# Linear recurrence of an adaLN network: one drive product per group, its halves exchanged through SBUF

## The reference, cut to what matters

```
h = layernorm(x) * (1 + ca) + sa
lam = exp(-exp(nu_log) + 1j*exp(theta_log))
Bu  = (h @ (B_re + 1j*B_im).T) * exp(gamma_log)      # 64 complex states per token
s_t = lam * s_(t-1) + Bu_t                            # along the 1024 tokens
y   = real(s @ (C_re + 1j*C_im).T) + h @ D.T
x   = x + ga * y
h   = layernorm(x) * (1 + cb) + sb
x   = x + gb * (shared_expert(h) + routed_experts(h)) # 8 experts, the best 2 of them
```

## Time and profile before

| what | value |
|---|---|
| median of 3 runs | 548.56 us (548.49 to 548.58) |
| the profiled execution | 549.87 us, its span 548.1 us |
| TensorE busy | 494.0 us (90%) |
| VectorE busy | 427.0 us (78%) |
| ScalarE busy | 349.6 us (64%) |
| GpSimd busy | 339.3 us (62%) |
| DMA | 20.98 MB moved, mean 38 GB/s |

### The profile page before, as it was taken

How to read it: one execution, slowest core, us unless ns; L and a number is a source line. 1 busy time by engine, 2 the same in 40 slices (tenths; PEclk the granted TensorE clock), 3 DMA queues, 4 the chain that set the end, 5 groups by cost and what they waited for, 6 DMA issues and landing times.

```text
span 548.1 us, 11812 instructions
## 1 busy us (share of the span) xinstructions
PE 494.0 (90%) x4059; PEld 315.8 (58%) x4059; DVE 427.0 (78%) x1173; ACT 349.6 (64%) x1001; POOL 339.3 (62%) x271
## 2 busy tenths in 40 slices
PE   5844088999999999999899999999999999999996
PEld 5424033567777776443467777777544445667775
DVE  6999999899888976566889988995545687566665
ACT  5854007699999987534679999998556526533332
POOL 5990028999999998668989999994111277410000
PEclk9975579999999999999989999999999999999999
DMA  8600003211111112000221111111000000000000
GB/s 300 238 1 1 0 3 109 56 39 32 40 40 41 41 39 71 0 2 0 77 49 35 37 41 39 41 40 31 1 1 0 0 1 1 1 1 19 22 20 19
DMA packets 15025, 20.98 MB, mean 38 GB/s; under 512 B 2379, under 2 KB 9013, under 8 KB 14709
## 3 DMA queue, kind: packets, MB, share of 16 engines
q1 hardware_dynamic: 14676, 20.13, 13.3%
q10 hardware_dynamic: 288, 0.08, 0.1%
HBM read 9.99 MB, written 1.05 MB: 20 GB/s over the span
## 4 chain that ended last, share of the span: by engine, by line
PE 68%; DVE 18%; POOL 6%; issue 4%; ACT 3%; DMA 1%; DVEq 0%; SPq 0%; POOLq 0%; ACTq 0%
PE psT L1523 11%; PE psQK L1615 9%; PE psO L1738 6%; PE psO L1670 5%; PE psQK L1945 5%; PE psS L1718 5%; DVE vst L1108 3%; DVE vAB L1112 3%; PE psO L1523 3%; PE psS L2017 3%; PE psQK L1752 3%; PE psO L2017 2%; PE psQK L1877 2%; PE psS L1854 2%; PE psQK L1756 2%
## 5 line engine op out<-in xcount | busy, mean ns | idle before, releaser
L576 ACT ACTIVATE prob<-psS,nmx 128x128 f32<-128x128 f32 x256 | 90.1, 378 | 18.2 <-DVE nmx L1248 18.2
L904 POOL TENSOR_TENSOR rn<-ssq,half 128x16 f32<-128x16 f32 x32 | 93.2, 2913 | 8.6 <-DVE ssq L1234 8.5
L896 POOL TENSOR_TENSOR ra<-ra,rb 128x512 f32<-128x512 f32 x64 | 81.0, 1286 | 1.0 <-DVE rb L1216 0.8
L716 POOL TENSOR_TENSOR rst<-mv,half 128x4 f32<-128x4 f32 x24 | 25.7, 1072 | 73.8 <-DVE mv L1009 64.2
L1615 PE MATMUL psQK<-wqkv,hsA 128*128 128x512 f32 x128 | 62.0, 604 | 1.0 <-DVE hsA L1197 0.6
L576 ACT ACTIVATION_READ_ACCUMULATOR prob<-psS,nmx 128x1 f32 x256 | 55.4, 216 | 0.0
L912 POOL TENSOR_TENSOR qkn<-ra,rn 128x512 f32<-128x512 f32 x32 | 49.0, 1532 | 2.5
L1213 DVE TENSOR_TENSOR ra<-psQK,rope 128x512 f32<-128x512 f32 x64 | 43.9, 686 | 7.5 <-PE psQK L1615 6.6
L1216 DVE TENSOR_TENSOR rb<-psQK,rope 128x512 f32<-128x512 f32 x64 | 43.5, 680 | 0.0
L697 ACT ACTIVATE gel<-psQK 128x512 f32<-128x512 f32 x32 | 19.1, 597 | 37.5 <-PE psQK L1945 37.5
L1227 DVE TENSOR_REDUCE ssq<-sq 128x8 f32<-128x512 f32 x64 | 41.1, 676 | 1.6 <-ACT sq L516 1.3
(11 more groups left out here) (263 smaller groups left out, 1177.6 us busy)
## 6 DMA issues: line engine op xcount, KB each, us to landing
vAB<-vAB SPq DMA_DIRECT2D x62, 128.0 KB, 2.2
wqkv<-in_wqkv SPq DMA_DIRECT2D x2, 768.0 KB, 8.2
big<-in_x SPq DMA_DIRECT2D x4, 256.0 KB, 5.3
ra<-in_rope_t SPq DMA_DIRECT2D x1, 1024.0 KB, 7.7
ropeb<-in_rope SPq DMA_DIRECT2D x1, 1024.0 KB, 8.6
big<-in_ew SPq DMA_DIRECT2D x2, 512.0 KB, 4.1
wmod<-in_wmod SPq DMA_DIRECT2D x2, 384.0 KB, 6.8
out<-big SPq DMA_DIRECT2D x3, 256.0 KB, 2.3
```

Source lines behind the costliest of these rows:

```text
L576: act.activation(prob[:, k, :], psS[:, hb, c * P:(c + 1) * P], ACT.Exp, bias=nmx[:, k:k + 1], accum_out=sums[:, n % 2, k:k + 1]).then_inc( ...
L896: pool.tensor_tensor(o, o, rb[:, r], ALU.add).then_inc(s["sum_" + name], 1)
L904: pool.tensor_tensor(rn[:, :], ssq[:, :], half[:, :], ALU.pow).then_inc(s["rn_ready"], 1)
```

## The change

One drive product per group is made instead of two. Its bank is psS for even groups and psO for odd ones (`lru_bank`). VectorE multiplies the bank by the cosine table as before. ScalarE then copies the bank's upper 64 partitions to the lower 64 of lru_half and the lower ones to the upper (`lru_swap`, two copies of 64 x 512), once VectorE has read the bank. GpSimd multiplies lru_half in place by the sine table and adds it to lru_in (`lru_add`, now two instructions). The product of z with the sine moves from GpSimd to VectorE, right behind the one with the cosine. The order of the calls changes with it: TensorE makes the drives of groups 0 and 1 together, drive 2 and the turn of norm (0,3) stand ahead of `lru_back(0)`, drive 3 right behind it; VectorE has the cosine products one place earlier; on ScalarE `lru_swap` 0 to 3 stand between the steps of the norms.

```diff
--- before.py
+++ after.py
@@ -197,7 +197,7 @@
             v_fill v_evac qT_fill qT_evac kT_fill kT_evac pT_fill pT_evac oT_fill oT_evac
             s_done negmax p_ready pv_done va_up0 va_up1 va_low0 va_low1 o_norm
             wo_done zmid hsM_ready g_mm a_mm gelu_done hg_done w2_done
-            bu_mm bu_half lru_g lru_m1 lru_m2 lru_a y_done xmid_ready
+            bu_mm bu_swap bu_half lru_g lru_m1 lru_m2 lru_a y_done xmid_ready
             rt_mm sig_done pairs_ready better_ready comb_ready sh_mm sh_act sh_h ey_done eh_mm eh_act ey_used acc_done
             gb_mm gb_ready wg_ready out_ready""".split()
         s = {n: sem(n) for n in names}
@@ -308,6 +308,7 @@
         lru_hn = [big[:, g, 0:GW] for g in range(NG)]
         lru_in = [ra[:, u * GW:(u + 1) * GW] for u in range(2)]
         lru_half = [rb[:, u * GW:(u + 1) * GW] for u in range(2)]
+        lru_bank = (psS[:, 0, :], psO[:, 0, :])
         lru_cos = [big[:, u, GW:2 * GW] for u in range(2)]
         lru_sin = [big[:, 2 + u, GW:2 * GW] for u in range(2)]
 
@@ -653,6 +654,14 @@
                 b = bof(g)
                 ln_out(late_ln(0, g), lru_hn[g], mod[:, 1, CA, b:b + 1], mod[:, 1, SA, b:b + 1])
 
+            def lru_swap(g):
+
+                act.wait_ge(s["bu_half"], g + 1)
+                if g >= 2:
+                    act.wait_ge(s["lru_a"], g - 1)
+                for p in (0, 64):
+                    act.activation(lru_half[g % 2][64 - p:128 - p, :], lru_bank[g % 2][p:p + 64, :], ACT.Copy).then_inc(s["bu_swap"], 1)
+
             def expert_out(g):
                 b = bof(g)
                 ln_out(late_ln(1, g), hsA[:, gsl(g)], mod[:, 1, CB, b:b + 1], mod[:, 1, SB, b:b + 1])
@@ -671,8 +680,15 @@
                     act.wait_ge(s["gb_mm"], 2)
                     act.activation(osb[:, 0:2 * P], psQK[:, 1, P:3 * P], ACT.Copy).then_inc(s["gb_ready"], 1)
                 ln_norm(late_ln(0, g))
+                if g == 2:
+                    lru_swap(0)
                 lru_out(g)
+                if g == 2:
+                    lru_swap(1)
+            lru_swap(2)
             for g in range(NG):
+                if g == 0:
+                    lru_swap(3)
                 ln_norm(late_ln(1, g))
                 if g >= 2:
                     shared_silu(g - 1)
@@ -950,28 +966,19 @@
 
             def lru_add(g):
 
-                pool.wait_ge(s["bu_half"], 2 * g + 2)
+                t = slice((g % GPB) * GW, (g % GPB + 1) * GW)
+                pool.wait_ge(s["bu_swap"], 2 * g + 2)
+                own.one(pool.tensor_tensor(lru_half[g % 2], lru_half[g % 2], tsin[:, t], ALU.mult))
+                pool.wait_ge(s["bu_half"], g + 1)
                 pool.tensor_tensor(lru_in[g % 2], lru_in[g % 2], lru_half[g % 2], ALU.add).then_inc(s["lru_a"], 1)
-
-            def lru_sine(g):
-
-                t = slice((g % GPB) * GW, (g % GPB + 1) * GW)
-                pool.wait_ge(s["lru_g"], g + 1)
-                if g >= 2:
-                    pool.wait_ge(s["y_done"], g - 1)
-                pool.tensor_tensor(lru_sin[g % 2], z[:, gsl(g)], tsin[:, t], ALU.mult).then_inc(s["lru_m2"], 1)
 
             lru_add(0)
             ln_rstd(late_ln(0, 3))
-            lru_sine(0)
             lru_add(1)
-            lru_sine(1)
             lru_add(2)
             ln_rstd(late_ln(1, 0))
-            lru_sine(2)
             lru_add(3)
             ln_rstd(late_ln(1, 1))
-            lru_sine(3)
             ln_rstd(late_ln(1, 2))
 
             def gate(b, count):
@@ -1386,15 +1393,12 @@
             def lru_products(g):
 
                 t = slice((g % GPB) * GW, (g % GPB + 1) * GW)
-                dve.wait_ge(s["bu_mm"], 2 * g + 1)
+                dve.wait_ge(s["bu_mm"], g + 1)
                 if g == 0:
                     dve.wait_ge(s["tabs_ready"], 2)
                 elif g >= 2:
                     dve.wait_ge(s["lru_g"], g - 1)
-                    dve.wait_ge(s["lru_a"], g - 1)
-                dve.tensor_tensor(lru_in[g % 2], psS[:, 0, :], tcos[:, t], ALU.mult).then_inc(s["bu_half"], 1)
-                dve.wait_ge(s["bu_mm"], 2 * g + 2)
-                dve.tensor_tensor(lru_half[g % 2], psO[:, 0, :], tsin[:, t], ALU.mult).then_inc(s["bu_half"], 1)
+                dve.tensor_tensor(lru_in[g % 2], lru_bank[g % 2], tcos[:, t], ALU.mult).then_inc(s["bu_half"], 1)
 
             def lru_scan(g):
 
@@ -1407,6 +1411,7 @@
                 if g >= 2:
                     dve.wait_ge(s["y_done"], g - 1)
                 dve.tensor_tensor(lru_cos[g % 2], z[:, gsl(g)], tcos[:, t], ALU.mult).then_inc(s["lru_m1"], 1)
+                dve.tensor_tensor(lru_sin[g % 2], z[:, gsl(g)], tsin[:, t], ALU.mult).then_inc(s["lru_m2"], 1)
 
             def lru_mixed(g):
 
@@ -1426,15 +1431,15 @@
 
             lru_products(0)
             ln(late_ln(0, 3))
+            lru_products(1)
             lru_scan(0)
-            lru_products(1)
+            lru_products(2)
             lru_mixed(0)
             lru_scan(1)
-            lru_products(2)
             ln(late_ln(1, 0))
+            lru_products(3)
             lru_mixed(1)
             lru_scan(2)
-            lru_products(3)
             ln(late_ln(1, 1))
             lru_mixed(2)
             lru_scan(3)
@@ -1903,10 +1908,9 @@
             def lru_drive(g):
 
                 pe.wait_ge(s["ln_out"], late_ln(0, g) + 1)
-                if g:
-                    pe.wait_ge(s["bu_half"], 2 * g)
-                mm(psS[:, 0, :], wlru[:, 0, :], lru_hn[g], start=True, stop=True).then_inc(s["bu_mm"], 1)
-                mm(psO[:, 0, :], wlru[:, 1, :], lru_hn[g], start=True, stop=True).then_inc(s["bu_mm"], 1)
+                if g >= 2:
+                    pe.wait_ge(s["bu_swap"], 2 * g - 2)
+                mm(lru_bank[g % 2], wlru[:, 0, :], lru_hn[g], start=True, stop=True).then_inc(s["bu_mm"], 1)
 
             def lru_direct(g):
 
@@ -1928,7 +1932,7 @@
                 g, j = divmod(k, 2)
                 pe.wait_ge(s["ln_out"], late_ln(1, g) + 1)
                 if k == 0:
-                    pe.wait_ge(s["bu_half"], 2 * NG)
+                    pe.wait_ge(s["bu_swap"], 2 * NG)
                 elif k == 3:
                     pe.wait_ge(s["ln_out"], late_ln(1, 2) + 1)
                 else:
@@ -1945,18 +1949,18 @@
                 mm(psQK[:, k % 2, :], ew1[:, e, :], hsA[:, gsl(g)], start=True, stop=True).then_inc(s["eh_mm"], 1)
 
             lru_drive(0)
+            lru_drive(1)
             late_t1(0, 3)
             lru_direct(0)
             ln_t2(late_ln(0, 2))
-            lru_drive(1)
             expert_gates()
+            lru_drive(2)
+            ln_t2(late_ln(0, 3))
             lru_back(0)
-            ln_t2(late_ln(0, 3))
-            lru_drive(2)
+            lru_drive(3)
             late_t1(1, 0)
             lru_direct(1)
             lru_back(1)
-            lru_drive(3)
             late_t1(1, 1)
             lru_direct(2)
             ln_t2(late_ln(1, 0))
```

## The result

The changed kernel takes 555.47 us, the median of 4 runs (555.03 to 556.95), against 548.52 (548.48 to 548.58) for the kernel before: a ratio of 1.0132 (95% interval 1.0115 to 1.0148), slower by 6.95 us. The direction was forecast, the size was not: 552.5, in a range that ended at 554.6.

What follows compares the result with a forecast made beforehand. TensorE, gapless from 453.5, ends as late as that point; VectorE's chain from `lru_mixed(0)` sets it. The last back product +4.0 us (3.44 removed included) turns 549.87 into 553.9; less 1.31 to the median, 552.5; range 549.6 to 554.6.

Steps and rivals of the forecast that it cites:

- scan 0: VectorE's scan of group 0, behind exchange, multiply and add: forecast to start at 441.85 instead of 439.98.
- the turn of norm (0,3): TensorE's transposes of norm (0,3): forecast at 444.65, practically where they stood before (444.52).
- TensorE idle for 3.6 us: Ahead of the turn at 444.65, TensorE was forecast to have only drive 2 and then nothing.
- the cosine of group 0 held by multiply 1: GpSimd's multiply 1 starts at 443.03, ahead of VectorE's cosine product (443.10), which is held to 444.15.
- The pair of copies: ScalarE's exchange, two 64x512 copies from PSUM: forecast 1.13 us for the two, 0.66 to 1.32 possible.
- most of TensorE's own saving would vanish: The later `lru_mixed(0)`, +2.3 us, was to use up two thirds of the 3.44 us in TensorE idle time.
- the step of `lru_back(0)`: TensorE's back products of group 0: start 445.09, end 447.01; the held sine, ending 445.44, still in time, price nil.
- mixed 0: VectorE's `lru_mixed(0)`, after the back products of group 0: forecast to go from 444.73 to 447.06, +2.3 us.
- Add 1 got in between cosine and sine: Rival, chance 0.13: GpSimd's add 1 between cosine 0 and sine 0, mixed 0 at 447.68, sine 1 later: +5.0, 553.6.
- the clock fell behind the idle time: Rival, chance 0.04: TensorE's clock falls after 3.6 us idle ahead of 444.65; for 5 us of work, +2.5: 555.0.
- From mixed 0 to the turn of expert norm 0: Recurrence after `lru_mixed(0)`: from 447.06 to TensorE's turn of expert norm 0 at 456.53 instead of 453.46, +3.1.
- the normalization of expert norm 0 wait for exchange 3: On ScalarE, exchange 3 stands ahead of it, 453.92 to 455.05; then 1.51 to the turn at 456.53.

Runs made afterwards that it cites:

- the run without the chain and with the old order: Changed kernel without exchange, multiply and add (sine half of the drive left out), `lru_back(0)` ahead of the turn of norm (0,3): 547.91 us, ratio 0.9987.
- the run where GpSimd waits: Changed kernel, but GpSimd starts multiply g (from 1) only when VectorE's sine product of group g - 1 is done: 553.96 us, ratio 1.0093.
- the run with both edits: Changed kernel with multiply g waiting for VectorE's sine product g - 1, and twelve constant products ahead of norm (0,3)'s turn on TensorE: 551.84 us, ratio 1.0053.
- back 0 first: Changed kernel with `lru_back(0)` ahead of the turn of norm (0,3) on TensorE, as before the change: 555.78 us, ratio 1.0133.
- the kernel before with the turn first: Kernel before, only with the turn of norm (0,3) ahead of `lru_back(0)` and drive 2 behind both: 551.89 us, ratio 1.0059.

## Why the prediction was wrong

**Right, with its mechanism.** From the first drive the prediction had scan 0 at 441.85 - 435.52 = 6.33 (measured 6.41), the turn of norm (0,3) at 9.13 (9.22), TensorE idle for 3.6 us (3.49) and the cosine of group 0 held by multiply 1 to about 1.7 us (1.72 for 0.69). By the page SBUF — State Buffer of the Trainium skill (Who interferes with whom) the first to start shuts the other out for its whole length, and the trace agrees here too. The pair of copies came out at 1.21 for 1.13. That most of TensorE's own saving would vanish is shown by the run without the chain and with the old order: at most 1.0 of 3.44 us is left.

**Wrong: the step of `lru_back(0)`.** It read: "Still in time for `lru_back(0)` at 445.09, so the price there is nil", and mixed 0 was put at 447.06, 11.54 behind the first drive. Measured is 13.24, 1.7 us more. Two terms that I had as rivals with a chance of 0.13 and 0.04 both came true in this step (of the first only this half: sine 1, which it had late as well, took 0.68). Add 1 got in between cosine and sine, so the second back product began at 445.34 (11.12 from the first drive, forecast 10.43): 0.7 us. And the clock fell behind the idle time, so that its record lasts 2.08 us instead of 1.02, and mixed 0 began 2.12 us after it instead of 1.11: 1.0 us. The two overlap: in the run where GpSimd waits, the half clock alone has the second product begin at 11.85. The split holds for this trace only. I had excused the clock with "behind well-filled stretches", which no row showed; the row that I had, half clock after 3.73 us of idle, was the better witness for an idle time of 3.6 us. So the failed step is this wait, priced at nil: with neither term, in the run with both edits, mixed 0 is at 11.66, 0.12 from the forecast.

**Mis-sized by less.** From mixed 0 to the turn of expert norm 0 I had 9.47 us (measured 9.76), from there to `shared_up(0)` 2.53 (2.87), and from there to the last back product's end 5.90 (6.11): 0.8 us more in sum. In the first, the prediction had the normalization of expert norm 0 wait for exchange 3, and the second step of the power done by then (454.65). In the trace exchange 3 ends at 455.09, and the normalization waits until 455.66 for that second step, which scan 2 holds: 1.20 us for 0.20. Part of the second is the same alternation in group 2, where both products were held (1.73 and 1.75) and the sine ended 0.39 us after TensorE was ready for it. With the 1.7 above the forecast of +4.0 becomes +6.5, the measured +6.4.

**Not seen.** GpSimd's multiply 0 also held a tiny `tensor_scalar` of 4 elements per partition on VectorE (L1015, 1.24 us for 0.17), in the statistics of norm (0,3). It cost nothing, as the power was queued behind add 0 anyway.

**What each part costs.** From the profiles, between the first drive and the end, each part as the difference of two neighbouring kernels: taking out the products, with the sine products of z on VectorE, brings -1.0; exchange, multiply and add, with no cosine or sine product held and at full clock, cost 115.2 - 111.5 = 3.7, and in that is what GpSimd's wait itself costs; the turn ahead of `lru_back(0)` 0.6; holding and clock together, less what the wait costs, 3.2. The sum is 6.4 by construction, so it confirms nothing. The medians give much the same steps: 547.91, 551.35, 551.84, 555.47 (the last is 3.6 there, as the changed kernel's profiled execution was its shortest). Of the 3.2 the share of each isn't a property of either: alone, removing the holding gives 1.9 and removing the idle time nothing. The order's 0.6 holds only where the other two are gone; in the kernel before, it costs 1.5 in the profile and more in the median.

## What to carry to other kernels

An engine busy for 91% of a stretch need not be its bound. Before removing its work, follow what the first result of the stretch waits for, and take out the work alone in an experiment: here 3.44 us removed were worth at most 1.0. Where a change lengthens a chain, look for what the new idle time does to TensorE's granted clock and for where two engines will now exclude each other, and price them together: a rival that is a consequence of the forecast's own idle time is no rival but a term. And when two engines alternate over one resource, it can pay to delay the one that isn't urgent: it gave 1.9 us net here, at the price of waits that show once the rest is gone.

## What was not expected of the hardware

- VectorE doesn't keep its turn for its next product: between two products that stood back to back without a wait, a GpSimd instruction got in and held the second one (1.72 and 1.75 us for 0.69), in group 0 of the changed kernel and again in group 2 (1.73 and 1.75). With GpSimd's wait none of them is above 0.69.
- A VectorE `tensor_scalar` with one input of 4 elements per partition was held too: 1.24 us beside a GpSimd multiply that began 0.04 earlier, 1.13 us twice more in the run with the sine product on GpSimd and 1.14 once in the run with back 0 first, 0.17 to 0.19 otherwise.
- The granted clock went to half in all four profiled kernels with 3.5 to 3.7 us of idle on TensorE, and at a different time in each, though the idle time begins 5.7 us behind the first drive in all: at 7.2 (back 0 first), 7.7 (sine product on GpSimd), 8.7 (GpSimd waits) and 10.2 us (changed kernel, where TensorE had been busy again for 1 us). It stayed low for 6.8 us in the first two and for 3.4 in the others, though TensorE worked nearly without a pause from the end of the idle time on. In the profile of the kernel before with the turn first, 2.44 us of idle left it at 1.00.
- Two copies of 64 x 512 from PSUM on ScalarE take 1.21 us together: half the partitions save nothing, as 128 x 512 lasts 0.66.
